# Softmax row maxima from the high parts of Q and K alone, two banks at a time in the row halves of the matmul array

## The reference, cut to what matters

```python
q = jnp.einsum('bsd,hde->bhse', x, Wq)          # B=4, S=1024, D=256, H=16, E=64; k and v alike
scores = jnp.einsum('bhse,bhte->bhst', q, k)
scores = jnp.where(causal, scores / jnp.sqrt(jnp.float32(E)), -jnp.inf)
attn = jax.nn.softmax(scores, axis=-1)
out = jnp.einsum('bhst,bhte->bhse', attn, v)
y = x + heads @ Wo                               # then a layer norm with gamma and beta
x = layernorm(x + y)
x = layernorm(x + ffn(x))                        # silu(x Wg) * (x Wu), times Wd; hidden 768
```

## Time and profile before

| | us |
|---|---|
| median of 3 runs | 1459.61 (1457.96 to 1460.11) |
| the profiled execution | 1458.47 |
| its span, first to last instruction | 1456.7 |
| TensorE busy | 1405.5 (96%) |
| VectorE, ScalarE, GpSimd busy | 1030.1, 1001.9, 985.7 |
| granted clock of TensorE, mean | 0.989 |

### The profile page before, as it was taken

The page is one execution under the profiler, slowest core; times in us unless marked ns, Lnnn a source line. Parts: engine busy times, 40 slices in busy tenths (PEclk is TensorE's granted clock), DMA queues, the critical chain, the costliest instruction groups (busy, mean ns, idle before and its releaser), DMA issues.

```text
span 1456.7 us, 23745 instructions
## 1 busy us (share of the span) xinstructions
PE 1405.5 (96%) x7936; PEld 1228.6 (84%) x7936; DVE 1030.1 (71%) x2747; ACT 1001.9 (69%) x1924; POOL 985.7 (68%) x926
## 2 busy tenths in 40 slices
PE   6999999999999999999999999999999999999977
PEld 5788888888888888888888888888888888888866
DVE  7777776767776766777667676776767677677874
ACT  4777777867676676867668676676767668676534
POOL 4665666556676775867768586775867768588744
PEclk9999999999999999999999999999999999999988
DMA  4323222313342132312233122132313223121000
GB/s 132 100 81 101 54 66 95 117 52 93 103 119 73 52 96 59 110 53 59 74 117 95 52 60 73 56 120 59 96 39 116 74 60 95 52 62 56 23 12 29
DMA packets 61240, 110.44 MB, mean 76 GB/s; under 512 B 16256, under 2 KB 41600, under 8 KB 61120
## 3 DMA queue, kind: packets, MB, share of 16 engines
q1 hardware_dynamic: 61120, 108.94, 25.0%
HBM read 60.95 MB, written 13.89 MB: 51 GB/s over the span
## 4 chain that ended last, share of the span: by engine, by line
PE 74%; ACT 11%; DVE 8%; POOL 4%; issue 3%; DMA 1%; ACTq 0%; SPq 0%; POOLq 0%
PE bank L797 23%; PE bank L770 15%; PE bank L670 8%; PE bank L746 8%; PE bank L733 7%; PE bank L695 5%; PE bank L832 5%; PE bank L844 3%; ACT probs_hi L982 2%; ACT probs L979 2%; POOL probs_lo L1423 2%; ACT y_tail L1018 1%; ACT Q L962 1%; ACT K L962 1%; POOL h_lo L1465 1%
## 5 line engine op out<-in xcount | busy, mean ns | idle before, releaser
L1423 POOL TENSOR_TENSOR probs_lo<-probs,probs_hi 128x512 fp32r<-128x512 f32 x576 | 747.4, 1305 | 417.4 <-ACT probs_hi L982 413.9
L979 ACT ACTIVATE probs<-bank 128x512 f32<-128x512 f32 x576 | 344.2, 598 | 302.3 <-DVE bank L1180 216.8
L770 PE MATMUL bank<-Q,K 128*128 128x512 f32 (+3 forms) x1536 | 386.3, 353 | 4.2 <-ACT probs_hi L982 4.1
L982 ACT ACTIVATE probs_hi<-bank 128x512 fp32r<-128x512 f32 x576 | 342.2, 594 | 0.0
L770 PEld LDWEIGHTS bank<-Q,K 128*128 128x128 f32 x1536 | 252.2, 190 | 34.7 <-ACT probs_hi L982 7.5
L746 PE MATMUL bank<-K,Q 128*128 128x512 f32 (+3 forms) x768 | 245.5, 362 | 2.7 <-DVE K L1131 2.1
L1164 DVE CUSTOM_DVE_ANT_0 bank<-bank,mask_keys_free 128x128 f32<-128x128 f32 (+3 forms) x512 | 242.9, 505 | 3.5 <-PE bank L746 3.0
L797 PE MATMUL bank<-probs_hi,VH 128*128 128x512 f32 (+3 forms) x768 | 232.7, 343 | 7.9 <-POOL probs_lo L1423 7.2
L797 PE MATMUL bank<-probs_lo,VH 128*128 128x512 f32 (+3 forms) x768 | 234.6, 346 | 0.0
L797 PE MATMUL bank<-probs_hi,VL 128*128 128x512 f32 (+3 forms) x768 | 234.5, 346 | 0.0
L1180 DVE TENSOR_TENSOR bank<-bank,mask_queries_free 128x256 f32<-128x256 f32 (+1 forms) x320 | 119.3, 373 | 130.6 <-PE bank L770 130.1
(11 more groups left out here) (171 smaller groups left out, 2220.0 us busy)
## 6 DMA issues: line engine op xcount, KB each, us to landing
Q<-Q SPq DMA_DIRECT2D x64, 256.0 KB, 3.7
K<-K SPq DMA_DIRECT2D x64, 256.0 KB, 3.6
recip_bc<-recip_scratch SPq DMA_DIRECT2D x62, 256.0 KB, 3.4
wh<-w_scratch SPq DMA_DIRECT2D x12, 768.0 KB, 4.3
wl<-w_scratch SPq DMA_DIRECT2D x12, 768.0 KB, 5.9
wo_quad<-wo SPq DMA_DIRECT2D x16, 256.0 KB, 3.2
y<-x SPq DMA_DIRECT2D x16, 256.0 KB, 3.8
x_tail<-x SPq DMA_DIRECT2D x13, 256.0 KB, 3.0
```

Of the source, the lines that this page charges most:

```text
L770: last = mm(bk[:, at:at + cols], KX[:, n, P * i:P * i + P], QX[:, n, q0:q0 + cols], start=(KX is K1 and at == 0), stop=(KX is K2 and at + ...
L979: A(pe_[:, g % 2, :], stb[g % 2][:, :], ACT.Exp).then_inc(exp_done, 1)
L982: A(ph[:, g % RING, :], stb[g % 2][:, :], ACT.Exp).then_inc(hi_done, 1)
L1423: G.tensor_tensor(pl[:, g % RING, :], pe_[:, g % 2, :], ph[:, g % RING, :].bitcast(F32), ALU.subtract).then_inc(lo_done, 1)
```

## The change

- A bank of the maximum pass is now made from the high parts alone, over 64 rows, in the half of the array where they lie: `K1` in the head's own half, or `K2`'s copy of K's high part with `Q1`'s copy of Q's in the other half.
- Banks 1 to 8 of a head go out in four pairs in one step of every two (`max_banks`), one bank in each half of the rows, their pieces interleaved; bank 0 goes alone. The pair waits for both PSUM banks. VectorE still reads one bank in each step (`max_reads`), in the steps where it did.
- So that K's copy lies in the other half, `K2` and `Q2` change their halves: the copy of K and the low part of Q go to the half that the head does not own, the row of the maxima and the ones to its own. VectorE writes Q's low part across halves now, as it did with K's.
- Bank 0 waits for K's high parts and no longer for the low parts and for Q's copy; the second bank of a pair waits for the copies of Q and K.
- TensorE issues the pass one step earlier (`MAX_LEAD` 14) and the transpose too (`T_LEAD` 4); SP issues the copy of K for heads 2 and 3 at step 4 instead of 5, ahead of a raw piece.

```diff
-MAX_LEAD = 13
-T_LEAD = 3
+MAX_LEAD = 14
+T_LEAD = 4
...
-EARLY_T = [12, 17]
+EARLY_T = [6, 12, 17]
+def max_early(g):
+    return [(NH - 2 + a, k) for a, k in EARLY_MAX.get(g - (NG - NST), [])]
 def max_due(g):
     h, k = divmod(g + MAX_LEAD, NS)
     if 0 <= h < NH - 2:
-        return [(h, k)]
-    return [(NH - 2 + a, k) for a, k in EARLY_MAX.get(g - (NG - NST), [])]
+        return [] if k % 2 else [(h, 0)] if k == 0 else [(h, k - 1), (h, k)]
+    return max_early(g)
+def max_reads(g):
+    h, k = divmod(g + MAX_LEAD - 1, NS)
+    return [(h, k)] * (0 <= h < NH - 2) + max_early(g)
...
-                sp.dma_start(bits(K2[0:E, a, :]), bits(K1[0:E, a, :])).then_inc(k_dup[pair], 16)
-                sp.dma_start(bits(K2[E:P, b, :]), bits(K1[E:P, b, :])).then_inc(k_dup[pair], 16)
+                sp.dma_start(bits(K2[E:P, a, :]), bits(K1[0:E, a, :])).then_inc(k_dup[pair], 16)
+                sp.dma_start(bits(K2[0:E, b, :]), bits(K1[E:P, b, :])).then_inc(k_dup[pair], 16)
...
-                row = E if n % 2 == 0 else 0
+                row = 0 if n % 2 == 0 else E
...
+                if s == 4 and live:
+                    dup_k(it, 1)
                 if has_pieces(it) and s in LOAD_RAW_AT:
...
-                if s == 5 and live:
-                    dup_k(it, 1)
...
+            def max_banks(due):
+                jobs = []
+                for place, (h, k) in enumerate(due):
+                    e, n = mx_event(h, k), h % QH
+                    if e >= 2:
+                        pe.wait_ge(mx_read, e - 1)
+                    if k == 0 and n % 2 == 0:
+                        pe.wait_ge(proj_hi, 2 * proj_unit(h // QH, n // 2, 3) + 2)
+                    copied = place == 1
+                    if copied:
+                        pe.wait_ge(q_dup[n // 2], 32 * (h // QH + 1))
+                        pe.wait_ge(k_dup[n // 2], 32 * (h // QH + 1))
+                    rows = slice(0, E) if (n % 2 == 0) != copied else slice(E, P)
+                    jobs.append((mxb[e % 2], rows, n, K2 if copied else K1, MAXB[k]))
+                for part in range(2):
+                    for bk, rows, n, KX, bank_pieces in jobs:
+                        if part < len(bank_pieces):
+                            at = sum(cols for _, _, cols in bank_pieces[:part])
+                            j, k0, cols = bank_pieces[part]
+                            last = mm(bk[:, at:at + cols], Q1[rows, n, P * j:P * j + P], KX[rows, n, k0:k0 + cols],
+                                      start=(at == 0), stop=(at + cols == CH))
+                last.then_inc(mx_mm, len(due))
...
-                        V.scalar_tensor_tensor(Q2[rows, hx, cols], bk[rows, :], SCALE,
+                        V.scalar_tensor_tensor(Q2[other, hx, cols], bk[rows, :], SCALE,
                                                Q1[rows, hx, cols].bitcast(F32), ALU.mult, ALU.subtract).then_inc(proj_lo, 1)
...
-                for h, k in max_due(g):
+                for h, k in max_reads(g):
                     max_bank(h, k)
```

More of the change, by code:

```diff
@@ L129, in max_due @@
     if 0 <= h < NH - 2:
-        return [(h, k)]
-    return [(NH - 2 + a, k) for a, k in EARLY_MAX.get(g - (NG - NST), [])]
+        return [] if k % 2 else [(h, 0)] if k == 0 else [(h, k - 1), (h, k)]
[3 more added lines that the diff above has]
+    return [(h, k)] * (0 <= h < NH - 2) + max_early(g)
 def transpose_due(g):
     if g - (NG - NST) in EARLY_T:
-        return NH - 2 + EARLY_T.index(g - (NG - NST))
+        return NH - 3 + EARLY_T.index(g - (NG - NST))
     h, rest = divmod(g + T_LEAD, NS)
-    return h if rest == 0 and 0 <= h < NH - 2 else None
+    return h if rest == 0 and 0 <= h < NH - 3 else None
 def mx_event(h, k):
@@ L576, in step @@
                     recip_load(QH * it)
-                if s == (EARLY_T[0] + 1 if it == NIT - 1 else 16) and live:
+                if s == (EARLY_T[1] + 1 if it == NIT - 1 else 16) and live:
                     max_to_row(QH * it + 2)
@@ L594, in step @@
                     recip_load(QH * it + 1)
-                if s == (EARLY_T[1] + 1 if it == NIT - 1 else 25) and live:
+                if s == (EARLY_T[2] + 1 if it == NIT - 1 else 25) and live:
                     max_to_row(QH * it + 3)
@@ L901, in step @@
                     max_transpose(transpose_due(g))
-                for h, k in max_due(g):
-                    max_bank(h, k)
+                if max_due(g):
+                    max_banks(max_due(g))
                 if 0 <= g - LAG < NG:
@@ L1124, in proj_rest @@
                     hx = 2 * pair + hd
+                    other = slice(E, P) if hd == 0 else slice(0, E)
                     dve.wait_ge(proj_hi, n + hd + 1)
                     if kind == 0:
-                        V.scalar_tensor_tensor(Q2[rows, hx, cols], bk[rows, :], SCALE,
+                        V.scalar_tensor_tensor(Q2[other, hx, cols], bk[rows, :], SCALE,
                                                Q1[rows, hx, cols].bitcast(F32), ALU.mult, ALU.subtract).then_inc(proj_lo, 1)
                     else:
-                        other = slice(E, P) if hd == 0 else slice(0, E)
                         V.tensor_tensor(K1[other, hx, cols], bk[rows, :],
@@ L1401, in _ @@
             for X in (Q2, K2):
-                V.memset(X[E:P, 0, :].bitcast(F32), 0.0)
-                last = V.memset(X[0:E, 1, :].bitcast(F32), 0.0)
+                V.memset(X[0:E, 0, :].bitcast(F32), 0.0)
+                last = V.memset(X[E:P, 1, :].bitcast(F32), 0.0)
             last.then_inc(zeros[0], 1)
@@ L1539, in _ @@
             pool.wait_ge(v_init, 1)
-            G.memset(Q2[E:P, 2, :].bitcast(F32), 0.0)
-            G.memset(K2[E:P, 2, :].bitcast(F32), 0.0).then_inc(rows_set, 1)
+            G.memset(Q2[0:E, 2, :].bitcast(F32), 0.0)
+            G.memset(K2[0:E, 2, :].bitcast(F32), 0.0).then_inc(rows_set, 1)
             pool.wait_ge(rows_set, 1)
-            G.memset(Q2[0:E, 3, :].bitcast(F32), 0.0)
-            G.memset(K2[0:E, 3, :].bitcast(F32), 0.0).then_inc(zeros[1], 1)
+            G.memset(Q2[E:P, 3, :].bitcast(F32), 0.0)
+            G.memset(K2[E:P, 3, :].bitcast(F32), 0.0).then_inc(zeros[1], 1)
             pool.wait_ge(zeros[0], 1)
@@ L1547, in _ @@
             for n in range(0, QH, 2):
-                G.memset(K2[E:E + 1, n, :].bitcast(F32), 1.0).then_inc(rows_set, 1)
+                G.memset(K2[0:1, n, :].bitcast(F32), 1.0).then_inc(rows_set, 1)
                 pool.wait_ge(rows_set, n + 2)
-                G.memset(K2[0:1, n + 1, :].bitcast(F32), 1.0).then_inc(rows_set, 1)
+                G.memset(K2[E:E + 1, n + 1, :].bitcast(F32), 1.0).then_inc(rows_set, 1)
                 pool.wait_ge(rows_set, n + 3)
```

## The result

| us | before | after |
|---|---|---|
| median | 1458.78 (1456.02 to 1460.11, 4 runs) | 1532.01 (1530.00 to 1534.06, 4 runs) |
| span of the profiled execution | 1456.7 | 1528.2 |
| granted clock, mean | 0.989 | 0.990 |

The change made the kernel slower: the ratio of the medians is 1.0508 (95% interval 1.0495 to 1.0520), 73.2 us. Forecast were 1441 us, and 1490 as the upper end.

The account below looks back on a forecast made before the run. TensorE was taken to bound the kernel, narrowly. Terms -58.9 + 3.2 + 33 + 3 + 1 = -18.7 us took the span-based 1458.5 to 1439.8, so a median of 1441 us; range 1404 to 1490.

Parts of the forecast that it names:

- The bound: Whole kernel: TensorE bounds it, but narrowly, with matmuls covering 96% of the span.
- The gain of 58.9 us: Maximum pass on TensorE: 576 banks become 320 slots at 0.23 us, 132.5 to 73.6 us.
- Rival 2: Maximum pass: the pairs do not run together, so TensorE gains nothing and new waits stay; 1490 us, chance 10%.
- The switch, 3.2 us: Around each of 320 maximum passes: leaving the full array and returning costs 0.01 us together, +3.2 us.
- Rival 1: Around the maximum passes: each of 640 switches drains the array, 0.11 or 0.27 us; 1508 or about 1614 us, chance 20%.
- Loading the second half's weights: In each pair: taken as 0 added, with a bound of 0.11 us a pair, 28 us in all.
- Waits in late iterations, 33 us: TensorE before the maximum pass: waits, mostly for VectorE's reads, 3.0 us in each of 11 iterations with a tail.
- 33 + 3 + 1: Added waits: 33 us in late iterations, 3 us in the five iterations before, 1 us at the start.
- rival 4: Steps without a maximum: GpSimd and the chain behind VectorE lose another 16 to 24 us; 1457 to 1465 us, chance 13%.
- The start, 1 us within 0 to 2.1: Kernel start: the pair waits for K's copy landing at 22.9, delaying the V projection; +1 us, most lost in later waits.
- The moves: Q's second factors crossing halves, K's copies earlier in SP's queue, transposes one step earlier: 0 or hidden past the start.

Follow-up runs that it names:

- e2: The changed kernel with both banks of a pair in the head's own 64 rows, one after the other; 1581.53 us, ratio 1.0853.
- e1: The changed kernel with every maximum bank over all 128 rows again, keeping the changed places; 1516.80 us, ratio 1.0404.
- e10: e1 with bank 0 of each head issued one step later; 1509.54 us, ratio 1.0348.
- e4: The kernel before, each maximum bank over its head's own 64 rows at its old place, no pairs; 1651.29 us, ratio 1.1344.
- e7: The kernel before plus a 128-column matmul over 128 rows and 32 array columns ahead of each maximum bank; 1499.84 us, ratio 1.0280.
- e8: The kernel before plus a 128-column matmul over 128 rows and 64 array columns ahead of each maximum bank; 1500.08 us, ratio 1.0286.
- e5: The kernel before plus a 128-column matmul over the full array ahead of each of the 576 maximum banks; 1502.70 us, ratio 1.0303.
- e9: The kernel before plus a 128-column matmul over 64 rows and 32 array columns ahead of each maximum bank; 1641.18 us, ratio 1.1252.
- e6: The kernel before plus a 128-column matmul over 64 rows and 128 array columns ahead of each maximum bank; 1685.02 us, ratio 1.1561.

## Why the prediction was wrong, by its steps

- **The bound** was right: TensorE sets the period, in the early iterations too; GpSimd's added wait equals the loss.
- **The gain of 58.9 us** was right as room on TensorE. e2 has 58.9 in bare passes and 49.5 in the time. (Rival 2, no overlap, makes 1492 by its terms, 1459.6 + 25 + 7, and not 1490; nothing hangs on it.)
- **The switch, 3.2 us, is the step that failed.** It measured 0.40 us a pass, 128 us. The bounds of the prediction, 0 to 0.54, held it; what was wrong was the value taken from the transpose as the "nearest" row. A change of columns was taken for one of rows, and the argument "a change of shape between the same neighbours" left out the very thing that differed. The rival's text had said it: "no row changes the number of rows". Emptying was put at 0.16 a change and measured about 0.09, loading at 0.11 and measured 0.11. Rival 1 was the mechanism, between its two prices (0.11 and 0.27 a change; 0.20 measured; 640 x 0.27 is 173 us, which makes 1611 and not 1614), over its point of decision (0.034), and was given 20% and left outside the range. That the measured 1532 lies between rival 1's two times is partly luck: the switches cost 128 us of TensorE's room, and added 65 to the time where nothing overlaps (e1 to e2). The rule of the Trainium skill named above spoke for it.
- **Loading the second half's weights** costs nothing more, as taken: the pair's matmuls start 0.003 to 0.004 us apart. The Trainium skill (TensorE: Matmul & The Clock Gate, "Part 3: Packing small matmuls — row/col tiling") has about 4 ns, and the trace agrees.
- **Waits in late iterations, 33 us.** Without switches (e1) steps 12 and 26 wait 0.99 and 1.12, nearly as worked out. In the changed kernel the same steps:

```profile
749.22 0.14 DVE L1185 DVE_READ_ACCUMULATOR2_ANT max_part<- 128x1 f32 x1
...
749.47 0.50 PE L768 MATMUL bank<-K,Q 64*128 64x512 f32 x2 [0.55 <-DVE max_part L1185]
...
787.76 0.14 DVE L1185 DVE_READ_ACCUMULATOR2_ANT max_part<- 128x1 f32 x1
...
788.01 0.52 PE L768 MATMUL bank<-K,Q 64*128 64x128 f32 x3 [0.74 <-DVE max_part L1185]
```

As room lost they are 0.62 and 0.78; with 0.33 in step 6 and 0.31 in two others the iteration has 2.0 us, not 3.0. The 0.5 of step 4 (K's high part) is not there, since TensorE arrives later: in the iteration from 720 us K's high part ends at 730.67 and the bank starts at 730.81. There are ten such iterations, not 11, since the last has no more than 0.2. And the kernel before had waits of its own, 1.5 us in a late iteration, which the forecast did not subtract; the largest, 0.73 in step 4, is gone. In the sum over the kernel, waits are 33.6 us against 32.8, so the net term is 1, not 36. The fault is the adding: a wait and a switch ahead of it cover each other (e1 to e2 above: 123.4 us of bare time added, 52.5 of waits gone). The other way round the term was too small: e10 has the places at 50.7 us without switches, where the prediction had 33 + 3 + 1 = 37. What it lacked are waits at the transpose (some 10 us more than before in e10) and in front of the first matmul of probabilities times V in steps without a maximum (19 more), for probs_lo among others; that chain is what rival 4 had in view.
- **The start, 1 us within 0 to 2.1**, measured 4.7 (first scores at 42.76 us, before at 38.05):

```profile
22.88 0.80 PE L768 MATMUL bank<-K,Q 64*128 64x512 f32 x3 [3.74 <-DMA K<-K]
23.60 0.58 PE L705 MATMUL bank<-wh,xh 128*128 128x256 f32 x1
```

  The landing at 22.9 was right, but the V projection behind the pair begins at 23.60, 2.8 later than in the earlier trace rows, beyond the bound; the 4.7 at the first scores show that none of it was made up in later waits; the passes ahead of them have switches too.
- **The moves** at nothing were right: the second factors of Q and of K take 689 ns each, and K's copy for heads 2 and 3 delays no pair in the middle; the wait for it is that of the start.
- **The size, put together:** bare passes +71.8, which are the 128 of the switch, -59 from running together, and some 3 for uneven pieces; waits +0.8. That is the 72.6 of the passes, beside 71.5 of span. Outside the passes TensorE loses 7 us at L818 in steps without a pass (8.5 against 1.6), and gets some 10 back ahead of the scores and of the tail's matmuls. The start's 4.7 is in part within these numbers; I did not take it apart.

What stays open: what the change would bring if a switch were free. No run can show it, since without the switch there is no pair. As an estimate, e10's 50.7 less e2's 49.5 is near no change, far from the -18.7 of the forecast; but those two prices were measured apart, and as the waits above show, such prices do not simply add.

## What to carry to other kernels

Before matmuls over part of the rows go between matmuls over all of them, count the excursions: here each cost 0.40 us, more than the 0.23 us that a pair of 512 columns saves, so it takes at least two pairs an excursion to gain, and the PSUM banks to hold them; what the new places cost comes on top (here some 50 us). When a price is taken from the nearest row, say in which property that row differs from the case, and give the rival a chance by that difference. Waits and stalls on one engine hide each other: sum them with both in place, and test a schedule without the new operation, since it alone may cost what the operation is to bring.

## What the runs showed of the hardware

- Changing between 128 and 64 rows costs TensorE 0.20 us each way (e4: 576 passes, 222 us of bare time). Changing between 128 and 32 or 64 columns costs nothing measurable (e7, e8 against e5: -2.9 and -2.6 us in 576 passes).
- With 32 columns of weights instead of 128 in the halves, a pass is 0.08 us shorter, and so is the load (0.10 in place of 0.18; e9 against e6).
- A full matmul of 128 columns put ahead of a bank costs more than its 0.06 us: the bank's weights no longer load behind it, and the slot of the next matmul is 0.285 us in place of 0.227 (e5). 0.12 x 576 = 69 us would follow; 44 were measured, in the main because the passes' waits fell from 33 to 18 us.
- Two matmuls in different halves of the rows start 0.003 to 0.004 us apart and take the time of one (e2 against after: 0.23 us a pair).
